# A decoder on one core: the first layer kept by features up to its output, and the joint stage's weight pieces in buffers of their own

## The reference

```python
x = hidden_states * rsqrt(mean(hidden_states ** 2) + eps) * norm_w
xz = x @ in_proj_w.T + in_proj_b                  # 512 -> 2 * 1536
x, z = xz[..., :Di], xz[..., Di:]
x = silu(causal_conv4(x) + conv_b)                # u below
xp = (x @ x_proj_w.T + x_proj_b).reshape(B, L, H, 1 + 2 * S)   # H 24, S 64
dt, Bs, Cs = xp[..., 0], xp[..., 1:1+S], xp[..., 1+S:]
Bs, Cs = Bs / norm(Bs), Cs / norm(Cs)
# alpha from dt, norm(Bs), mean of u over the head; then, per head and token t:
h = alpha * h + (1 - alpha) * B_t x_t             # 64 x 64 state
y_t = C_t h
out = (Y * silu(z)) @ out_proj_w.T + out_proj_b
x1 = layernorm(x + x + res_gate * out)
```

## Time and profile before

| | us |
|---|---|
| median of three runs | 5150.24 |
| profiled execution | 5107.47 |
| its span, first to last instruction | 5105.8 |
| TensorE busy | 4036.0 (79%) |
| VectorE busy | 2823.3 (55%) |
| ScalarE busy | 1618.9 (32%) |
| POOL busy | 1412.4 (28%) |
| both weight pieces of a unit (1536 KB), issue to landing | 5.9 |
| mean DMA rate | 118 GB/s |

### The profile page before, as it was taken

How to read it: one execution, slowest core, us unless ns; L and a number is a source line. 1 busy time by engine, 2 the same in 40 slices (tenths; PEclk the granted TensorE clock), 3 DMA queues, 4 the chain that set the end, 5 groups by cost and what they waited for, 6 DMA issues and landing times. The chain is left out here.

```text
span 5105.8 us, 61033 instructions
## 1 busy us (share of the span) xinstructions
PE 4036.0 (79%) x19166; PEld 3090.8 (61%) x19166; DVE 2823.3 (55%) x5022; ACT 1618.9 (32%) x3311; POOL 1412.4 (28%) x1213
## 2 busy tenths in 40 slices
PE   7985999979999796852995886677778778837993
PEld 6874777767777544642442775455556556715772
DVE  6664344443444344972223674899999855532335
ACT  4342222232222110020221565555555422203431
POOL 0001200000000003755102440899999800011002
PEclk9997999989999898965997898898889989968996
DMA  4224622232122343133996534332222021133324
GB/s 129 104 100 175 198 81 79 65 103 83 58 86 74 109 187 129 45 142 103 339 318 223 167 121 150 117 138 93 82 79 78 28 99 52 49 97 112 116 95 120
DMA packets 434226, 603.28 MB, mean 118 GB/s; under 512 B 115142, under 2 KB 310791, under 8 KB 424849
## 3 DMA queue, kind: packets, MB, share of 16 engines
q1 hardware_dynamic: 388240, 490.99, 29.3%
q0 software_dynamic: 43232, 101.96, 6.0%
q10 hardware_dynamic: 2592, 8.39, 0.4%
HBM read 436.56 MB, written 206.54 MB: 126 GB/s over the span
## 5 line engine op out<-in xcount | busy, mean ns | idle before, releaser
L2216 PE MATMUL d_py<-d_h,d_ident 128*128 128x256 f32 x2048 | 543.5, 425 | 176.4 <-POOL d_h L2056 156.7
L2064 POOL TENSOR_TENSOR d_dBu<-d_B,d_dtu 128x1024 f32<-128x1024 f32 x256 | 596.8, 2362 | 115.4 <-DMA d_dtu<-dtu 115.4
L2216 PEld LDWEIGHTS d_py<-d_h,d_ident 128*128 128x128 f32 x2048 | 431.1, 214 | 288.3 <-POOL d_h L2056 184.6
L715 PE MATMUL a_pB<-a_uhi,a_whi 128*128 128x512 f32 x1152 | 487.7, 423 | 40.9 <-DVE a_ulo L598 40.8
L715 PE MATMUL a_pB<-a_uhi,a_wlo 128*128 128x512 f32 x1152 | 461.6, 401 | 0.0
L715 PE MATMUL a_pB<-a_ulo,a_whi 128*128 128x512 f32 x1152 | 458.7, 398 | 0.0
L2102 ACT ACTIVATE d_ph<-d_dt,d_A 128x255 f32<-128x255 f32 x1024 | 425.7, 460 | 0.1
L2162 DVE TENSOR_TENSOR_SCAN d_ph<-d_ph,d_dBu 128x1024 f32<-128x1024 f32 x160 | 365.7, 2286 | 18.4 <-POOL d_dBu L2064 12.0
L1004 POOL TENSOR_TENSOR b_kv<-b_c 128x128 f32 (+11 forms) x256 | 100.3, 431 | 864.6 <-DMA b_c<-ctx_turned 860.7
L715 PEld LDWEIGHTS a_pB<-a_uhi,a_whi 128*128 128x128 f32 x1152 | 223.4, 194 | 83.3 <-issue 31.7
L682 DVE SCALAR_TENSOR_TENSOR a_W<-a_pG,a_cB,a_M 128x256 f32<-128x256 f32 (+1 forms) x384 | 142.7, 413 | 229.7 <-PE a_pG L736 129.9
(11 more groups left out here) (459 smaller groups left out, 9409.5 us busy)
## 6 DMA issues: line engine op xcount, KB each, us to landing
c_gu<-w_gu SPq DMA_DIRECT2D x64, 768.0 KB, 5.1
a_wraw<-w_bc SPq DMA_DIRECT2D x24, 1536.0 KB, 5.9
a_alall<-alpha SPq DMA_DIRECT2D x24, 1024.0 KB, 5.9
slots<-a_zeros POOLq DMA_DIRECT2D x64, 256.0 KB, 3.4
c_wd<-w_down SPq DMA_DIRECT2D x64, 256.0 KB, 6.1
c_xb<-slots SPq DMA_DIRECT2D x64, 256.0 KB, 8.0
slots_y<-c_y POOLq DMA_DIRECT2D x64, 256.0 KB, 7.1
f_w1r<-w SPq DMA_DIRECT2D x64, 256.0 KB, 2.6
```

The lines of the kernel that those rows point to most:

```text
L715: ins = nc.tensor.matmul(out, a[:, k, cols], b[:, k, ts], start=(k == 0 and n == 0), stop=(k == F - 1 and n == 2))
L2064: pool.tensor_tensor(dBu[c % RB][:, :, :], B_sb[i][:, q * G:(q + 1) * G, :], dtu_sb[i][:, f, :].unsqueeze(1).to_broadcast([P, G, L]), ALU. ...
L2216: ins = nc.tensor.matmul(py[f % 2][:, 0:L], ident_sb[:, :], h_sb[c % RH][:, n, :], start=False, stop=(q == Q - 1 and n == G - 1))
```

## The change

- `ssm0_project` projects z as it does x, by features, 12 blocks of 256 tokens; ScalarE adds the bias with silu; z is stored by features.
- `ssm0_scan`: u comes in 24 chunks through six buffers; B's and C's weight pieces have one buffer, half as big, and are loaded apart; constants are loaded after the 18th chunk; the output has u stationary (64 columns, a head each) and W moving, so that y comes by features; W has four buffers; rC goes to memory and back, spread over partitions; each clearing store waits for the one before; in the first step of the second half B's 24 projections lie between the output's pieces.
- `ssm0_out` reads y and z by features, splits y z and the weights in high and low parts, multiplies with three products, turns nothing but the result, and writes it into the tile that `long_conv` works on. Nothing is stored.
- `long_conv` loads no x, the first filter ahead of the context, the context in four pieces.
- `mix_project`: a buffer for each of the 16 weight chunks (in the memory of u and z), `DT_AT` 4 in place of 3.

```diff
@@ ssm0_project
+                        act.wait_ge(s_pz, b * F + g + 1)
+                        nc.scalar.activation(z_sb[:, g, :], pz[g % 2][:, 0:L], ACT.Silu, bias=bz_sb[:, g:g + 1]).then_inc(s_z, 1)
-                        nc.vector.tensor_tensor(zb[n % 2][:, :], pz[n % 2][:, :], bz_sb[:, (n % 3) * BANK:(n % 3 + 1) * BANK], ALU.add).then_inc(s_zb, 1)
+                    for k in range(KD):
+                        ins = parts(pz[f % 2][:, 0:L], (w_hi, w_lo), slice(DI + f * P, DI + (f + 1) * P), (xnT_hi, xnT_lo), slice(0, L), k)
@@ ssm0_scan, SP
+            def c_weights(pair, unit):
+                sp.wait_ge(s_wl, unit * 2 + 1)
+                sp.dma_start(w_raw[:, :, :], w_bc[bass.ds(pair, 1), :, :, C_COLS].rearrange("a p k n -> (a p) k n")).then_inc(s_w, 16)
+            def consts():
+                sp.wait_ge(s_ul, UCH - UBUF)
...
+            def norms(cur):
+                sp.wait_ge(s_rC, cur + 1)
+                sp.dma_start(norm_rows.rearrange("r t -> t r"), rC[:, :, :].rearrange("p h c -> p (h c)"), allow_slow_non_contiguous=True).then_inc(s_rC_stored, 16)
+                sp.wait_ge(s_rC_stored, cur * 16 + 16)
+                for h in range(2):
+                    sp.dma_start(rC_all[h * S:(h + 1) * S, :], norm_rows[h * TT:(h + 1) * TT, :].rearrange("c t -> (c t)").partition_broadcast(S)).then_inc(s_rC_all, 16)
             def step(half, cur, nxt, parity=None, first=False):
+                if cur is not None:
+                    norms(cur)
...
-                        weights(0 if last else pair + 1, nxt + 1, 1 - into)
+                        b_weights(0 if last else pair + 1, 1 - into)
                     if not first:
                         spread(nxt, into)
+                    if parity is not None or nxt < UNITS - 1:
+                        c_weights(0 if last else pair + 1, nxt + 1)
@@ ssm0_scan, VectorE and TensorE
+                    if i >= 3 and i % 2 == 1 or i == NI:
+                        b = (i - 3) // 2 if i < NI else NBH - 1
+                        if b == 0:
+                            dve.wait_ge(s_rC_all, cur * 32 + 32)
+                        nc.vector.tensor_tensor(y_sb[:, b * L:(b + 1) * L], py[:, 0:L], rC_all[:, b * L:(b + 1) * L], ALU.mult).then_inc(s_ye, 1)
-                    nc.tensor.matmul(py[:, o:o + S], W[i % 2][:, 0:P], u0, start=True, stop=True)
-                    nc.tensor.matmul(py[:, o + S:o + 2 * S], W[i % 2][:, P:2 * P], u0, start=True, stop=False)
-                    nc.tensor.matmul(py[:, o + S:o + 2 * S], W[i % 2][:, 2 * P:3 * P], u1, start=False, stop=True).then_inc(s_y, 1)
+                    for lo, w0, w1, c, start, stop in ((0, 0, P, 0, True, True), (P, P, 2 * P, 0, True, False), (P, 2 * P, 3 * P, 1, False, True)):
+                        for h in range(2):
+                            r = slice(h * S, (h + 1) * S)
+                            ins = nc.tensor.matmul(py[r, lo:lo + P], ut_sb[at][:, 2 * b + c, r], W[(2 * b + h) % 4][:, w0:w1], start=start, stop=stop)
+                if first:
+                    for j in range(BLK * F):
+                        slots[j // (BLK * F // NI) + 1].append(j)
@@ ssm0_out
+            load(0, 0)
+            for k in range(F):
+                if k >= WBUF:
+                    sp.wait_ge(s_wl, k - WBUF + 1)
+                sp.dma_start(w_raw[k % WBUF][:, :], w_out[k * P:(k + 1) * P, :]).then_inc(s_w[k % WBUF], 16)
+            load(1, 1)
...
-                        ins = nc.tensor.matmul(po[c][:, :], yT[:, c, k, :], w_sb[:, k, :], start=(k == 0), stop=(k == F - 1))
+                        for n, (v, w) in enumerate(((y_hi[i], w_hi), (y_hi[i], w_lo), (y_lo[i], w_hi))):
+                            ins = nc.tensor.matmul(po[c][:, :], v[:, k, at], w[:, k, :], start=(k == 0 and n == 0), stop=(k == F - 1 and n == 2))
@@ long_conv
-            sp.dma_start(x_sb[:, :, :], x_feat.rearrange("k p t -> p k t")).then_inc(s_x, 16)
+            filters(0, 0)
@@ mix_project
-    SMALL_AT, DT_AT = 2, 3
+    SMALL_AT, DT_AT = 2, 4
+        w_raw = [t[:, f:f + 2, :].rearrange("p f t -> p (f t)") for t in u_sb + z_sb for f in range(0, F1, 2)]
```

More of the change, by code:

```diff
@@ L94, in ssm0_project @@
         ut_sb = m.sb("ut", [P, 2, DI])
-        zb = [m.sb(f"zb{i}", [P, BANK]) for i in range(2)]
-        z_sb = m.sb("z", [P, 2, DI])
+        z_sb = m.sb("z", [P, F, L])
         pT = m.ps("pT", (P, 2, BANK))
@@ L477, in step @@
                                  .rearrange("(c p) n -> p c n", p=P)).then_inc(s_ut, 16)
+                    if first and half == 0:
+                        consts()
                     sp.wait_ge(s_wl, nxt * 2 + 2)
@@ L764, in project @@
                         ins.then_inc(s_pB, 1)
-                    if k == 3 and n >= 1:
-                        if n == 1 and cur is not None:
+                    late = first and cur is not None and n <= 2
+                    if k == 3 and n >= 1 and not (late and n == 1):
+                        if n == (2 if late else 1) and cur is not None:
                             pe.wait_ge(s_rootC, nxt)
+                        if n == 1 and cur is None:
+                            pe.wait_ge(s_first, 32)
                         if n == BLK + 1:
                             pe.wait_ge(s_arg, nxt + 1)
+                        if late:
+                            norms(nxt, 0)
                         norms(nxt, n - 1)
@@ L791, in step @@
                             scores(i // 2 + 1)
-                        output(i)
+                        if i % 2 == 1:
+                            output(i // 2)
                 if first:
-                    for j in range(NQ * F):
+                    for j in range(BLK * F, NQ * F):
                         project(j)
@@ L807, in ssm0_out @@
         m = Space(nc, "a3", phase)
-        w_sb = m.sb("w", [P, F, D])
+        WBUF = 4
+        w_raw = [m.sb(f"wraw{i}", [P, D]) for i in range(WBUF)]
+        w_hi, w_lo = (m.sb("w" + n, [P, F, D], F32R) for n in ("hi", "lo"))
         ident_sb = m.sb("ident", [P, P])
@@ L834, in pipelined, with ahead @@
                     products(2 * r + 1 + i, r + i, (1 + i) % 2)
-                    norm(2 * r + i, i)
+                    norm(2 * r + i, i, r)
             products(NB - 1, NB // 2 - 1, 1)
             for i in range(2):
-                norm(NB - 2 + i, i)
+                norm(NB - 2 + i, i, NB // 2 - 1)
+        def ahead(eng, products, norm):
+            for i in range(2):
+                products(i, 0, i)
+            with eng.Fori(0, NB // 2 - 1) as r:
+                for i in range(2):
+                    norm(2 * r + i, i, r, lambda r=r, i=i: products(2 * r + 2 + i, r + 1, i))
+            for i in range(2):
+                norm(NB - 2 + i, i, NB // 2 - 1, None)
         def rows(a, b, n):
@@ L853, in store @@
-            def store(b):
-                sp.wait_ge(s_oT, b * 2 + 2)
-                alone(sp, tick_sp)
-                sp.dma_start(rows(x1, b, L), o_sb[:, :, :]).then_inc(s_out, 16)
-                for c in range(2):
-                    sp.dma_start(x1_feat[:, :, bass.ds(b * L + c * P, P)].rearrange("k p t -> p k t"), oT[:, c, :, :]).then_inc(s_out, 16)
-            for i in range(2):
-                load(i, i)
-            with sp.Fori(0, NB // 2 - 1) as r:
-                for i in range(2):
-                    b = 2 * r + i
+                for dst, src in ((y_sb, y_feat), (z_sb, z_feat)):
+                    sp.dma_start(dst[i][:, :, :], src[:, :, bass.ds(b * L, L)].rearrange("k p t -> p k t")).then_inc(s_in[i], 16)
@@ new lines, in residual @@
+            def residual(b, i):
+                sp.dma_start(x_sb[i][:, :, :], rows(x, b, L)).then_inc(s_x[i], 16)
+            load(0, 0)
[4 more added lines that the diff above has]
+            load(1, 1)
+            for i in range(2):
+                residual(i, i)
+            sp.wait_ge(s_yl, 2)
+            load(2, 0)
@@ L864, in _ @@
+            for b in range(NB):
+                if b + 3 < NB:
+                    sp.wait_ge(s_yl, b * 2 + 4)
+                    alone(sp, tick_sp)
+                    load(b + 3, (b + 1) % 2)
+                if b + 2 < NB:
                     sp.wait_ge(s_ln, b * 2 + 2)
                     alone(sp, tick_sp)
-                    load(b + 2, i)
-                    store(b)
-            for i in range(2):
-                store(NB - 2 + i)
-            sp.wait_ge(s_out, NB * 48)
+                    residual(b + 2, b % 2)
```

294 lines of the change are left out of this document (143 added, 151 removed).

## The result

The changed kernel takes 5037.25 us (median of four runs, 5034.78 to 5041.8); the kernel before, on the same chip, 5149.86 (four runs, 5148.37 to 5150.84). The ratio is 0.978, with a 95% interval of 0.9765 to 0.9796: 112.6 us less, where 130 were forecast (5020, range 4978 to 5072).

What follows compares the result with a forecast made beforehand. TensorE's own work was taken to bound the scan and output projection. Terms of -14 - 42 - 14 + 9 - 61 - 6 - 2 = -130 us took the median of 5150.2 to 5020 us, range 4978 to 5072.

Steps and rivals of the forecast that it cites:

- I take that difference as unchanged: Base of the sum: the median stays 42.8 us above the profiled execution, so 4978 us profiled gives 5020.
- The scan's usual step: Scan: one output covering both heads, with W's waits gone, saves 1.9 us in each of 22 steps, -42 us.
- rival 1: Scan output: the two heads run in series, the step term is +4 in place of -42, 5066 us; chance 0.22.
- Rival 2: Scan: the array changes tiles at no cost and the starts go well, -71 in place of -42, 4985 us; chance 0.14.
- The round trip of C's norms: Scan's usual steps: norms go to memory and back, hidden with 4 us to spare, cost 0.
- The start: Start of the scan: TensorE starts where it did, splits end near 481, preparation starts near 487; -14 us.
- Between the halves: Scan's step between its halves: B's projections lie between the outputs, -14 us (bounds -5, -22).
- Last unit: End of the scan: the norms' round trip is bare there, +9 us (bounds +3, +12).
- The input projection: z by features: same columns through the array, ScalarE's and VectorE's changes don't set the pace; 0, within 5 us either way.
- The output projection: Output stage: split-format products without y's transposes, 17.6 us a batch in place of 26.0; -61 us (bounds -45, -68).
- Rival 4: Output stage: bound by its loads, y and z coming in 1 KB pieces; +15, 5035 us; chance 0.08.
- The joint stage: Joint stage: weight chunks' own buffers -5, step sizes one block later +3 (bounds -15, +10); together -2 us.

Runs made afterwards that it cites:

- experiment 1: The kernel before, profiled a second time with no edit: 5151.61 us, where its first profiled execution took 5107.47.
- experiment 9: The kernel before, with C's last norms of a unit put behind the first three projections of the next: 5095.82 us, ratio 0.9912.
- 6: experiment 2 plus the 80 clearing stores issued by GpSimd in the input projection in place of the scan's first half: 4964.79 us, ratio 0.9647.
- experiment 3: The changed kernel, with head 0's three output products issued ahead of head 1's in place of alternating: 5035.2 us, ratio 0.9771.
- experiment 2: The changed kernel, with C's last norms behind the next unit's first three projections in the 22 usual steps: 5000.68 us, ratio 0.9708.
- Experiment 8: The changed kernel with `DT_AT` back at 3, step sizes of the joint stage from block 3 on: 5048.88 us, ratio 0.9801.

## Why the prediction was right, and where it was off

**The sum.** -130 was forecast, -112.6 measured by the medians and -115 by the second profile of before. That it came so near is in part luck. Against that profile the input projection, the start, the usual steps, the boundary, the output projection, the long convolution and the routing came out 36 us worse than forecast together, the last unit, the joint stage, the experts and what stands behind them 21 us better, 17 of it in the joint stage.

**The profiled execution as a base.** The step "I take that difference as unchanged" was wrong: a profile of 4978 us was forecast and 5036.4 came, because the 42.8 us were no property of profiling. They were 28.6 us in routing, where the first profile alone has no stops, and 14.2 in the joint stage (experiment 1). The median of 5020 stood because it was the median that the sum was taken from.

**The scan's usual step: -42, measured -27.** The mechanism and the size of the edit held: 0.39 us a batch and its waits were to give 1.9 us a step, and experiment 9 against 6 measures 1.97. The two column halves overlap as the scores' row halves do: 0.81 us where rival 1 asked for 1.28, so rival 1 is out, and experiment 3 shows that the overlap hangs on the order. Rival 2 is out too: the 0.09 and 0.10 us around an output stay. What failed is "22 x 1.9 = -42". A step of 49.1 us was a mean of steps of 48.5 and 50.1, the latter with a fall of the clock behind the 1.36 us wait, in 9 of 22. I carried that mean on. The shorter step has the fall in 19 of 22, which gives back 10 x 1.5 us: -27 in place of -42.

**The round trip of C's norms: 0.** Right for the changed kernel: in its usual steps no output waits for y. The 4 us to spare were real and small: in the step shown above the loads go out at 837.98, land some 4 us after their issue (the median of these loads in the trace) and y is taken out at 846.91. With experiment 2 they were gone in the first half, and TensorE stood 24.5 us there.

**The start: -14, measured -9.6** (bounds 0, -20). "TensorE starts where it did" failed: it starts 24.6 us into the stage in place of 21.7, since C's weights are asked for only when B's are split and both come ahead of u. The last split ends at 493.3, not 481, 0.82 us of wait for ScalarE's conversion just ahead of it; VectorE first uses the constants at 496.34, not 487. Of these 12 and 9 us 5.3 are the later start of the stage (445.3 in place of 440.0), so the start itself lost some 4 us against the forecast. **Between the halves: -14, measured -10.6**, inside the bounds. **Last unit: +9, measured +7.1.** The store goes out at 1663.92, the loads at 1674.53, 10.6 us later (10.8 taken from alpha's), and the first y comes 16.0 us behind the clamp (15 forecast).

**The input projection: 0, measured +5 to +7**, just past the bounds. What failed is "neither sets the pace between batches". TensorE now waits 2.04 us a batch for ScalarE's silu of z, which stands behind the next batch's sum of squares and root and their table loads (ScalarE, 202.09 to 206.48):

```profile
207.01 0.39 PE L300 MATMUL a_pz<-a_xnThi,a_whi 128*128 128x256 f32 x1 [2.04 <-ACT a_z L212]
```

With the 0.8 us that it still waits for u that makes 2.85 us, against 1.21 and 1.02 us of waits for u before: 0.6 us more a batch. The period grew from 51.1 to 51.9 us.

**The output projection: -61, measured -58.4.** The period is 17.68 us, forecast 17.6; TensorE stands 10.06 us ahead of batch 1, forecast 6. The period before was 25.2 us and not the 26.0 of the window, so eight batches gave 60 us and not 67; start and end together cost some 2 us where 6 were forecast. Rival 4 is out: y times z waits for z only in batches 0 and 1. **Long convolution: -6, measured -5.5.**

**The joint stage: -2, measured -18.7** against the second profile of before, -4.5 against the first. What failed is "TensorE is not what closes this loop", hence +3 for the later step sizes. Experiment 8 puts them at -9 to -18 by one profile (441.1 us against 423.0 to 432.3), and its waits point to TensorE's wait for dt, which stood in front of a projection that ScalarE was about to need. It was priced by the waiting engine's own line and not by who queues behind.

## What to carry to other kernels

A mean step length can hide two kinds of steps: list every repetition before multiplying, and ask whether each short wait of TensorE also costs the clock behind it. Here 1.36 us of wait cost up to 3.2 (48.1 against 44.9), and removing it with what then stood in its way (experiments 2 and 6) gave some 70 us, three fifths of what the whole change gave. A memory round trip that is hidden by 4 us is only hidden at today's step length and today's DMA load. And compare a profile with the median stage by stage, not as one number: 43 us sat in two stages, between two profiles of one and the same kernel.

## What the runs showed of the hardware

- Column tiles of TensorE: an output of both heads, alternating, takes 0.81 us to the next matmul, head by head 1.07 (experiment 3); in series it would be 1.28, an estimate from single records. The Trainium skill (TensorEngine Tiling (Array Packing), Key Properties) says that different tiles can execute in parallel; the runs agree, with a factor of 1.6 against that estimate, and show that the order of issue decides how much of it is had.
- How often the clock fell behind the same wait of 1.36 us differed from kernel to kernel, and not in the order of the step's length: in 9 or 10 of 22 steps where a step without the fall takes 48.5 us (before), in 2 where 47.6 (experiment 3), in 19 where 46.5 (the changed kernel). Without the wait it fell in none (experiments 6 and 9).
- Beside 128 indirect stores from GpSimd, 1.29 us from one to the next, VectorE stood 42 to 69 us in one stage in eleven of twelve profiles, at instructions that wait for TensorE, which had ended; beside plain stores from the same queue, at 234 GB/s in place of 93, and without stores it did not, in one profile each.
